# GpSimd takes over the small operations of a layer norm, and VectorE takes its row sums in halves

## What is computed

```python
xn = (x - mean(x)) / sqrt(var(x) + 1e-5)
Q, K, V = relu(xn @ Wq + bq), relu(xn @ Wk + bk), relu(xn @ Wv + bv)      # 16 heads of 16
mask = sign(abs(sum(xn, axis=-1)))                                        # of a row, as key and as query
attn = softmax(where(causal and mask of the key, Q K^T / 4, -2**32)) * mask of the query
a = attn @ V + xn ; a = gamma * layernorm(a) + beta
ffn = shared_expert(xn) + sum over the 2 best of 8 experts(xn), weighted
out = x + a + ffn
```

## Time and profile before

| | us |
|---|---|
| median of 3 runs (lowest, highest) | 2234.32 (2233.48, 2238.47) |
| the profiled execution | 2235.82 |
| its span, first to last instruction | 2234.1 |
| busy in it: TensorE, VectorE, ScalarE, GpSimd | 1916.0, 1399.5, 1080.4, 1123.0 |
| mean granted TensorE clock | 0.945 of full |
| first phase, pass -3 to the barrier | about 10 to 1150 |
| passes 0 to 12 | 161.5 to 981.5 |
| median and profiled execution apart | 1.5 |

### The profile page before, as it was taken

How to read it: one execution, slowest core, us unless ns; L and a number is a source line. 1 busy time by engine, 2 the same in 40 slices (tenths; PEclk the granted TensorE clock), 3 DMA queues, 4 the chain that set the end, 5 groups by cost and what they waited for, 6 DMA issues and landing times. The chain is left out here.

```text
span 2234.1 us, 37281 instructions
## 1 busy us (share of the span) xinstructions
PE 1916.0 (86%) x13238; PEld 1378.0 (62%) x13238; DVE 1399.5 (63%) x2934; ACT 1080.4 (48%) x2048; POOL 1123.0 (50%) x935
## 2 busy tenths in 40 slices
PE   0478988898898888889658999999999999799997
PEld 0245544554455544455327888888888888577776
DVE  6577788778877787877404656565555633355554
ACT  0115555555455555555335666666666654122221
POOL 5444433544455434542324767777776753544331
PEclk9769999999999999999878999999999999899999
DMA  1654565566666665666254666666566653444341
GB/s 36 120 98 80 105 115 115 128 127 125 120 134 130 127 122 127 123 119 125 80 178 162 203 207 206 208 195 207 188 209 200 212 179 99 137 142 135 115 128 57
DMA packets 235375, 314.01 MB, mean 141 GB/s; under 512 B 18970, under 2 KB 200356, under 8 KB 229028
## 3 DMA queue, kind: packets, MB, share of 16 engines
q1 hardware_dynamic: 222948, 278.63, 50.2%
q0 software_dynamic: 12288, 33.57, 5.0%
HBM read 211.43 MB, written 100.70 MB: 140 GB/s over the span
## 5 line engine op out<-in xcount | busy, mean ns | idle before, releaser
L495 ACT ACTIVATE pT<-st_ps 128x512 f32<-128x512 f32 (+1 forms) x704 | 383.6, 559 | 481.7 <-PE st_ps L995 396.6
L1638 PE MATMUL gu<-xc,w_up_h 128*128 128x512 f32 x1760 | 556.2, 397 | 41.1 <-DVE hf L1528 18.7
L719 DVE TENSOR_REDUCE mx<-s_ps 128x1 f32<-128x512 f32 (+3 forms) x704 | 436.1, 637 | 157.5 <-PE s_ps L974 125.8
L972 PE MATMUL s_ps<-k_aug,q_aug 97*128 97x512 bf16 (+3 forms) x1024 | 296.5, 322 | 138.4 <-DVE mx L719 128.4
L1638 PEld LDWEIGHTS gu<-xc,w_up_h 128*128 128x128 f32 x1760 | 324.9, 190 | 127.7 <-issue 34.3
L1638 PE MATMUL gu<-xc,w_up_l 128*128 128x512 f32 x880 | 345.9, 393 | 0.4 <-issue 0.3
L1360 POOL TENSOR_TENSOR w_up_l<-w_raw,w_up_h 128x512 fp32r<-128x512 f32 x160 | 204.1, 1298 | 209.2 <-ACT w_up_h L1442 209.2
L993 PE MATMUL st_ps<-q_aug,k_aug 99*128 99x512 bf16 (+3 forms) x1024 | 288.2, 314 | 21.9 <-ACT pT L495 11.4
L972 PEld LDWEIGHTS s_ps<-k_aug,q_aug 97*128 97x128 bf16 x1024 | 102.6, 101 | 323.2 <-DVE mx L719 237.3
L1528 DVE TENSOR_TENSOR hf<-sil,gu 128x512 f32<-128x512 f32 x220 | 150.9, 686 | 231.3 <-ACT sil L1447 230.6
L411 POOL DMA_INDIRECT expert_rows<-xrow,slot x128 | 125.2, 978 | 314.9 <-DMA q_aug<-neg_scr 248.1
(11 more groups left out here) (206 smaller groups left out, 3423.5 us busy)
## 6 DMA issues: line engine op xcount, KB each, us to landing
w_raw<-in_L_ffn_w_dram SPq DMA_DIRECT2D x117, 512.0 KB, 6.1
part_scr<-parts SPq DMA_DIRECT2D x64, 384.0 KB, 9.4
q_aug<-part_scr SPq DMA_DIRECT2D x192, 128.0 KB
k_aug<-part_scr SPq DMA_DIRECT2D x192, 128.0 KB
xr<-expert_rows SPq DMA_DIRECT2D x39, 512.0 KB
expert_results<-yo SPq DMA_DIRECT2D x39, 512.0 KB, 3.3
x_sb<-in_L_attn_x_dram SPq DMA_DIRECT2D x16, 512.0 KB
layernorm_rows<-xn SPq DMA_DIRECT2D x16, 512.0 KB
```

The costliest lines, as they stand in the source:

```text
L495: fn(pT[:, j % 2, h:h + heads, 0:w], unit_view(st_ps[u % 2], heads, w), ACT.Exp).then_inc(exp_done, 1)
L719: vec.tensor_reduce(mx[:, q, h:h + heads], unit_view(s_ps[u % 2], heads, keys), AX_X, ALU.max).then_inc(s_max, 2)
L972: mm(v[:, n], q_aug[par][0:ROWS_S, h0 + n, P * q:P * (q + 1)], k_aug[par][0:ROWS_S, h0 + n, 0:keys], start=True, stop=False)
L1638: last = mm(gu[m % 2][:, a], w_up[wpar][x][:, a, c, P * m:P * (m + 1)], xc[par][:, y, c], start=k == 0, stop=k == 3 * NC - 1)
```

## The change

It moves the 128x4 arithmetic of the norm and the folds from VectorE to GpSimd, in six pieces: `small_mean` (fold and mean), `small_variance` (fold, mean, epsilon and the power), `small_step`, `small_root`, `small_parts` and `small_mask`. VectorE keeps the wide operations, the reciprocals (which it alone does here) and the bit masks. Every passing of the work between the two is a semaphore of its own. VectorE's three row sums become six instructions of half the width, each in a unit of its own. The units move: sums of x after 1 and 2, centring 4 (was 3), squares 13 and 14 (was 14), reciprocals 18, 20 and 23 (the root was at 18 and 20), quotient 25 and 27 (was 24 and 26), masks 40, 41 and 43 (was 41 and 42). Two fused operations (multiply and add in one) become two each on GpSimd, since it takes a tensor operand for every constant (`norm_consts`). `xn_ready` is renamed `mk_ready`.

```diff
-        AT_NORM = (1, 2, 3, 14, 15, 18, 20, 24, 26, 41, 42)
+        AT_MEAN, AT_CENTRE, AT_VAR = (1, 2), 4, (13, 14)
+        AT_R0, AT_R1, AT_RD, AT_QUOT, AT_BITS = 18, 20, 23, 25, 27
+        AT_MASKS = (40, 41, 43)
...
+            small_begin, small_mark, small_op, small_end = chain(pool, chain_small, 28)
+
+            def fold4(a, b, final):
+                small_op(gp.tensor_tensor(tree2[:], a, b, ALU.add))
+                t2 = tree2[:].rearrange("p t (a b) -> p t a b", b=2)
+                small_op(gp.tensor_tensor(tree3[:], t2[:, :, :, 0], t2[:, :, :, 1], ALU.add))
+                return gp.tensor_tensor(final, tree3[:, :, 0], tree3[:, :, 1], ALU.add)
...
+            def small_mean(b):
+                small_begin(b)
+                await_(pool, mean_part, 2 * (b + 1))
+                small_op(fold16(s[SUM]))
+                await_(pool, a_ready, b)
+                gp.tensor_tensor(s[MEAN], s[SUM], inverse, ALU.mult).then_inc(mean_ready, 1)
+
+            def small_variance(b):
+                await_(pool, var_part, 2 * (b + 1))
+                small_op(fold4(lanes[:, :, 0:4], lanes[:, :, 4:8], s[SUM]))
+                small_op(gp.tensor_tensor(s[T1], s[SUM], inverse, ALU.mult))
+                small_op(gp.tensor_tensor(s[V1], s[T1], eps, ALU.add))
+                gp.tensor_tensor(s[S0], s[V1], half[:], ALU.pow).then_inc(s1_ready, 1)
+
+            def small_step(b):
+
+                await_(pool, r0_ready, b + 1)
+                small_op(gp.tensor_tensor(s[Q1], s[V1], s[R0], ALU.mult))
+                small_op(gp.tensor_tensor(s[T1], s[Q1], s[S0], ALU.add))
+                gp.tensor_tensor(s[D1], s[T1], half[:], ALU.mult).then_inc(d1_ready, 1)
+
+            def small_root(b):
+
+                await_(pool, r1_ready, b + 1)
+                small_mark(gp.tensor_tensor(s[SL], s[D1], s[SH], ALU.subtract))
...
+                gp.tensor_tensor(s[ROOT], s[T1], s[D1], ALU.add).then_inc(root_ready, 1)
+
+            def small_parts(b):
+                await_(pool, root_ready, b + 1)
+                await_(pool, rd_ready, b + 1)
+                small_mark(gp.tensor_tensor(s[DL], s[ROOT], s[DH], ALU.subtract))
+                small_op(gp.tensor_tensor(s[NRD], s[RD], minus, ALU.mult))
+
+            def small_mask(b):
+                await_(pool, mask_part, 2 * (b + 1))
+                await_(pool, mk_ready, b)
+                fold16(s[MASK_SUM]).then_inc(mask_sum, 1)
+                small_end()
```

`fold16` is two additions and then `fold4`, five operations; `small_root` has eleven. Their places in GpSimd's `body`:

```diff
+                if norm:
+                    small_mean(i + 3)
                 for b in mine if one is None else []:
                     scatter(b, range(NT))
...
                 if norm:
-                    await_(pool, v1_ready, i + 4)
-                    gp.tensor_tensor(sm[:, 2], sm[:, 1], half[:], ALU.pow).then_inc(s1_ready, 1)
+                    small_variance(i + 3)
                 if project:
                     second(i + 2, 2)
+                if norm:
+                    small_step(i + 3)
                 if project:
                     second(i + 2, 3)
                     third(i + 2, 2)
+                if norm:
+                    small_root(i + 3)
                 if one is not None:
                     scatter(one, [2])
                 if project:
                     third(i + 2, 3)
                 if norm:
+                    small_parts(i + 3)
                     quotient(i + 3)
                 if one is not None:
                     scatter(one, [3])
+                if norm:
+                    small_mask(i + 3)
```

On VectorE:

```diff
+            def row_sums(rows_, h):
+
+                t_ = slice(2 * h, 2 * h + 2)
+                return vec.tensor_reduce(lanes[:, t_], rows_[:, t_].rearrange("p t (k l) -> p t l k", l=16), AX_X,
+                                         ALU.add)
+
+            def ln_mean(b, h):
+                if h == 0:
+                    await_(dve, x_in, 16 * (b + 1))
+                    await_(dve, mask_sum, b)
+                row_sums(x_sb, h).then_inc(mean_part, 1)
...
             def ln_centre(b):
-                ln(vec.tensor_scalar(sm[:, MEAN], sm[:, SUM], 1.0 / C, None, ALU.mult))
+                await_(dve, mean_ready, b + 1)
+                await_(dve, normed, b)
...
+            def ln_r0(b):
                 await_(dve, s1_ready, b + 1)
...
+                vec.reciprocal(s[R0], s[S0]).then_inc(r0_ready, 1)
+
+            def ln_r1(b):
+                await_(dve, d1_ready, b + 1)
+                vec.reciprocal(s[R1], s[D1])
+                vec.tensor_scalar(s[SH].bitcast(U32), s[D1].bitcast(U32), HIGH_BITS, None, ALU.bitwise_and
+                                  ).then_inc(r1_ready, 1)
+
+            def ln_rd(b):
+                await_(dve, root_ready, b + 1)
+                vec.reciprocal(s[RD], s[ROOT])
+                vec.tensor_scalar(s[DH].bitcast(U32), s[ROOT].bitcast(U32), HIGH_BITS, None, ALU.bitwise_and
+                                  ).then_inc(rd_ready, 1)
...
+            def ln_masks(b, h):
+                if h == 0:
+                    await_(dve, normed, b + 1)
+                row_sums(xn, h).then_inc(mask_part, 1)
...
             def ln_masks_end(b):
-                fold(lanes[:], sm[:, SUM], ln)
-                ln(vec.tensor_scalar(msk[:], sm[:, SUM], 0.0, None, ALU.not_equal))
+                mask_begin(b)
+                await_(dve, mask_sum, b + 1)
+                mask(vec.tensor_scalar(msk[:], s[MASK_SUM], 0.0, None, ALU.not_equal))
                 await_(dve, mk_ps, b)
```

More of the change, by code:

```diff
@@ L106, in attention_phase @@
         cmask = sb("cmask", [P, 2, P], BF16)
-        half = sb("half", [P, NT])
+        half, norm_consts = sb("half", [P, NT]), sb("norm_consts", [P, 3, NT])
         zeros = sb("zeros", [P, NT, C])
@@ L383, in _ @@
             gp.memset(one[:], 1.0).then_inc(consts, 1)
-            await_(pool, consts, 4)
+            for k, value in enumerate((1.0 / C, LN1_EPS, -1.0)):
+                gp.memset(norm_consts[:, k], value).then_inc(consts, 1)
+            await_(pool, consts, 7)
             gp.affine_select(out=identf[:], in_=identf[:], compare_op=ALU.is_equal, fill=0.0, base=0,
@@ L424, in third @@
                 gp.tensor_tensor(parts[:, 2, u], r1[:, u], parts[:, 1, u], ALU.subtract).then_inc(b2_done, 1)
+            s = [sm[:, k] for k in range(20)]
+            inverse, eps, minus = (norm_consts[:, k] for k in range(3))
+            small_begin, small_mark, small_op, small_end = chain(pool, chain_small, 28)
[4 more added lines that the diff above has]
+                return gp.tensor_tensor(final, tree3[:, :, 0], tree3[:, :, 1], ALU.add)
@@ new lines, in fold16 @@
+            def fold16(final):
+                v = lanes[:].rearrange("p t (a b) -> p t a b", b=4)
+                t1 = tree1[:].rearrange("p t (a b) -> p t a b", b=4)
+                small_mark(gp.tensor_tensor(t1[:, :, 0], v[:, :, 0], v[:, :, 1], ALU.add))
+                small_op(gp.tensor_tensor(t1[:, :, 1], v[:, :, 2], v[:, :, 3], ALU.add))
+                return fold4(t1[:, :, 0], t1[:, :, 1], final)
+            def small_mean(b):
[4 more added lines that the diff above has]
+                gp.tensor_tensor(s[MEAN], s[SUM], inverse, ALU.mult).then_inc(mean_ready, 1)
@@ new lines, in small_root @@
+            def small_root(b):
+                await_(pool, r1_ready, b + 1)
+                small_mark(gp.tensor_tensor(s[SL], s[D1], s[SH], ALU.subtract))
+                small_op(gp.tensor_tensor(s[REM], s[SH], s[SH], ALU.mult))
+                small_op(gp.tensor_tensor(s[T2], s[V1], s[REM], ALU.subtract))
+                small_op(gp.tensor_tensor(s[REM], s[SH], s[SL], ALU.mult))
+                small_op(gp.tensor_tensor(s[T1], s[REM], s[REM], ALU.add))
+                small_op(gp.tensor_tensor(s[T3], s[T2], s[T1], ALU.subtract))
+                small_op(gp.tensor_tensor(s[T2], s[SL], s[SL], ALU.mult))
+                small_op(gp.tensor_tensor(s[REM], s[T3], s[T2], ALU.subtract))
+                small_op(gp.tensor_tensor(s[T3], s[REM], s[R1], ALU.mult))
+                small_op(gp.tensor_tensor(s[T1], s[T3], half[:], ALU.mult))
+                gp.tensor_tensor(s[ROOT], s[T1], s[D1], ALU.add).then_inc(root_ready, 1)
@@ L647, in _ @@
-            s = [sm[:, k] for k in range(20)]
-            def ln_root(b):
-                await_(dve, s1_ready, b + 1)
-                ln(vec.reciprocal(s[R0], s[S0]))
-                ln(vec.tensor_tensor(s[Q1], s[V1], s[R0], ALU.mult))
-                ln(vec.tensor_tensor(s[T1], s[Q1], s[S0], ALU.add))
-                ln(vec.tensor_scalar(s[D1], s[T1], 0.5, None, ALU.mult))
-                ln_mark(vec.reciprocal(s[R1], s[D1]))
-                ln(vec.tensor_scalar(s[SH].bitcast(U32), s[D1].bitcast(U32), HIGH_BITS, None, ALU.bitwise_and))
@@ L675, in ln_quotient @@
             def ln_quotient(b):
+                ln_begin(b)
+                await_(dve, rd_ready, b + 1)
                 for i in range(NT):
@@ L678, in ln_quotient @@
                 ln(last)
```

(21 more changed lines are left out.)

104 lines of the change are left out of this document (36 added, 68 removed).

## The result

The changed kernel takes 2230.08 us, the median of 14 runs (2225.76 to 2235.58), against 2236.7 us for 14 runs of the kernel before that were taken with them. The ratio is 0.9969 with a 95% interval of 0.9958 to 0.998: faster by 0.31%, some 7 us. The forecast was 1.2%, 27 us. The sign and the range held; three quarters of the gain did not come.

What follows compares the result with a forecast made beforehand. No single engine bounds a pass: VectorE its ends, TensorE most units, a GpSimd chain units 13 to 17. Ten passes 17.5 us, early passes 10, pass -1 1, start -4, clock 2: 27 us off, 2207 us, range 2188 to 2238.

Steps and rivals of the forecast that it cites:

- The price of a link: One small chained operation on GpSimd costs 0.28 us with its pause, ends 0.28 and 0.46; on VectorE about 0.20.
- rival (a): GpSimd's links are longer than four trace rows say; at 0.46 us each, about 2252 us in all; chance 0.16.
- The wait at the mean: Units 0 to 4: VectorE waits 0.55 us for `mean_ready`, 1.75 us after the second half, two maxima covering 1.2.
- The pass's ends: Units 40 to 43 gain 0.9 us a pass; units 0 to 4 between nothing and 0.57, taken as 0.35.
- The cast of unit 17: Units 13 to 17: `second(2)` 0.7 us late, VectorE's cast back from 1.37 to 0.43 us; net gain 0.2.
- Passes 0 to 2 and the start: Passes without scatters gain about 3.4 us each, 2.2 in units 18 to 22; the unhidden first norm costs about 4.
- Units 5 to 12 ... are TensorE's: In the typical pass TensorE bounds units 5 to 12, busy 10.20 of 11.13 us; no gain or loss entered.
- Units 23 to 26: Gain of 0.3 us a pass, as two small operations go on to unit 23.
- Units 18 to 22: Some 3.3 us of VectorE's small operations leave or move on; TensorE bounds the typical pass, so no gain here.
- (b): TensorE's low-clock stretches fill what is given back; only units 40 to 43 and early passes pay: 2226 us, chance 0.14.
- (c): VectorE's relief of 6.6 us ends the low-clock stretches, passes near 57.8 us: 2186 us in all, chance 0.12.
- (d): VectorE isn't relieved, waiting for GpSimd as long as it worked; half so at unit 4, counted inside (a).

Runs made afterwards that it cites:

- first two experiments: GpSimd's scatter 0 and its wait moved from the stream's head to just before the quotient: on the changed kernel 2205.84 us, on the kernel before 2241.35 us.
- second experiment: Kernel before, with GpSimd's scatter 0 and its wait moved to just before the quotient: 2241.35 us, ratio 0.9991.
- eighth experiment: Kernel before with negated maxima loaded first on SyncE, scatters 0 and 1 heading GpSimd's stream, scatter 2 behind `third(3)`: 2167.3 us, ratio 0.995.
- third experiment: Changed kernel with GpSimd's scatter 2 put behind `third(3)` instead of ahead of it: 2226.38 us, ratio 0.9913.
- first and fourth experiments: Changed kernel, with scatter 0 moved to just before the quotient: 2205.84 us; with SyncE's negated maxima ahead of its fourteen loads: 2205.36 us.
- seventh experiment: Changed kernel with negated maxima loaded first on SyncE, scatters 0 and 1 heading GpSimd's stream, scatter 2 behind `third(3)`: 2110.51 us, ratio 0.969.

## Why the prediction held, and where it failed

The mechanism of the gain was right, and its price too. What the forecast lacked was a wait that the gain itself would bring about, and a collision.

**The price of a link: right.** It was put at 0.28 us with its pause. After, by line over 100 to 982 us (busy, mean ns | idle before):

```profile
L439 POOL TENSOR_TENSOR tree<-tree 128x8 f32<-128x8 f32 x43 | 8.7, 202 | 3.4
L445 POOL TENSOR_TENSOR tree<-lanes 128x16 f32<-128x16 f32 x29 | 6.4, 219 | 86.1 <-DVE lanes L692 84.0 <-issue 2.1
```

202 ns and 0.08 before each; with 16 columns 219, and 0.27 on average for the dearest (L489). The first link of a chain costs no more than the others, so rival (a), for which the 0.38 of the earlier trace rows spoke, is out.

**The wait at the mean: right in size.** Forecast 0.55 us:

```profile
719.26 0.22 POOL L445 TENSOR_TENSOR tree<-lanes 128x16 f32<-128x16 f32 x1 [4.47 <-DVE lanes L692]
...
720.83 1.14 DVE L705 TENSOR_SCALAR ln_a<-x_sb,sm 128x256 f32<-128x256 f32 x4 [0.46 <-POOL sm L454]
```

The six links take 719.26 to 720.80, the wait is 0.46. What was not seen is that the halves create it: a second half in unit 2 is done one unit later than a whole sum in unit 1. With whole sums the wait is gone and the stage takes 5.95 us. The second instruction of a split sum costs 0.14 us (2.01 against 1.87), not "at most 0.1".

**The pass's ends: right in kind, too small in size.** Units 40 to 43 were put at -0.9 and gave -1.14; units 0 to 4 at -0.35 and gave -0.84, more than the 0.57 that was to be the most. The step from 0.57 to 0.35 was taken for the low clock of 0.77; after, the granted clock in these units is 1.00. Where the rest above 0.57 comes from I have not traced.

**The cast of unit 17: right.** It came down from 1.37 to 0.42 us:

```profile
746.52 0.42 DVE L769 CAST parts<-r 128x512 bf16<-128x512 f32 x1
```

The net of -0.2 for units 13 to 17 can't be read off the changed kernel: they start 3.6 us late, GpSimd's chain having had that time, and take 8.72 us at a clock of 0.81. The first two experiments show it, since scatter 0 is out of the way in both: 10.34 us with the change and 10.65 without it, -0.3.

**Passes 0 to 2 and the start: right.** 3.4 us each was said and 4.0 measured; the stretch of units 18 to 22 that was to lose 2.2 of its 8.74 us lost 3.1 (8.74 to 5.68). The start was to cost 4; the first unit of pass -1 came 4.8 later (102.1 to 106.9). Pass -1 gave back 3.6, where 1 was said.

**"Units 5 to 12 ... are TensorE's": the step that failed.** It was true of pass 8 of the kernel before, and was carried over as if it would stay true, with nothing put down for these units in the sum. I cut units 5 to 12 as one stretch, saw 10.20 of 11.13 us busy, and listed the waits of the engines that were late, not of those that were early. GpSimd's 194.4 us of waiting for `neg_loaded` (ten times, up to 23.5 us) was in the same view as the earlier trace rows:

```profile
POOL expert_rows L411 <- DMA q_aug<-neg_scr: 194.4, 10, 23.5
```

It looked like the idle time of an engine that isn't the bound. It is in fact the end of a chain of 17.5 us that starts at one point of the pass and is awaited at another, with a slack of 1.41 us at `second(1)` and none at `second(0)`. The forecast took 1.25 us out of the pass around these two points (0.9 and 0.35) and nearly 2 came (1.14 and 0.84), and it never asked what would wait when the work got there earlier.

The loss can be added up, from pass 8 before to pass 9 after, of which this is the stretch of units 10 to 12:

```profile
728.71:736.84 8.13, 4.50 (x42) 2.39 (x39) 2.87 (x5) 4.59 (x9) 4.53 (x5) 0.96 0.54 163
```

It is 3.8 us longer than the 4.33 of before. VectorE's cast of unit 11 starts 6.38 us after unit 10 (728.71 to 735.09) instead of 3.48 (679.43 to 682.91), so 2.9 later. Of these, 1.7 come from the start of the chain, which now falls 1.7 us and not 3.4 ahead of the pass; 0.8 from units 0 to 9, which take 13.3 us instead of 14.1; 0.4 from the chain itself. The last 0.9 is the cast, 1.36 us instead of the 0.43 of the earlier trace rows: `second(1)` no longer has to wait for `qf` and runs beside it. On GpSimd the slack absorbs its share: `second(1)` starts 1.4 us late (6.3 us after unit 10, at 735.0, instead of 4.9), so that a part of the 3.8 us is made up for in units 13 to 17, which hang on GpSimd. Removing the chain gave back 2.0 to 2.2 us a pass (63.26 to 61.23 and 61.11).

The kernel before had shown the chain at work. Its pass 13, the one without a norm, lost some 4 us to it. These are units 10 to 12 of that pass, in the kernel before and in the same kernel with scatter 0 moved (second experiment):

```profile
992.58:1001.07 8.49, 4.49 (x42) 2.39 (x39) 2.87 (x5) 4.59 (x9) 4.50 (x5) 0.94 0.28 95
```

```profile
995.05:999.37 4.32, 4.32 (x42) 2.40 (x39) 2.01 (x4) 3.05 (x6) 1.15 (x1) 1.00 0.32 107
```

So the pass that the prediction took as its cap, 57.8 us, had some 4 us of the very chain in it that then took the gain. With the order mended and no other change, pass 13 takes 52.2 us (eighth experiment), and full passes with the change get below the supposed cap (57.0 with whole sums).

**Units 23 to 26: wrong sign.** 0.3 us of gain was put there. The text saw that `third(3)` would come up to 3 us later and asked only who reads its tile. It did not ask what would run beside it. That costs 1.05 us in this pass, some 10 us in all; the third experiment gives it back.

**Units 18 to 22: too careful.** Put at nothing for the typical pass on account of the clock of 0.77; they gave 1.64, at 1.00. The caution was not groundless: with the chain out of the way the low clock is back there in half of the passes (first and fourth experiments).

**VectorE's busy time: down by 77 us, not by about 100.** Of the difference 15 us are the quotient's multiplies, which are held up beside `third(3)` (29.7 us after, 14.7 before).

**The rivals.** (b) named 2226 and 8 us of gain, and the whole time is close to it, but not for its reason: the granted clock over passes 3 to 12 rose from 0.94 to 0.96, the time was lost in units 10 to 12 and 23 to 26, and edits of order brought it back. That the number fits is luck. Its mechanism exists, though: where only the chain was removed, the lower clock took 1.5 us of units 18 to 22 back in half of the passes. (c), passes near 57.8 us, is what the change gives with all three edits of order (57.8 in the seventh experiment), and the low-clock stretches go with it, as (c) had it: the granted clock over passes 3 to 12 is 0.99. (d), VectorE waiting for GpSimd, came true in form, 44.1 us of waiting for `r`; but GpSimd was itself waiting for a DMA and not at work.

**What stays open.** Pass 13 took 57.9 us before, 59.9 after, 63.2 with scatter 2 moved and 53.3 with the negated maxima first. The 2 us between the first two are the chain again (units 10 to 12 take 8.49 before and 10.43 after), but in some runs units 27 to 39 of this pass take 17.1 to 17.5 us instead of 13.9, and pass 14 lost 1.9 (70.5 to 72.4); neither is traced. Scatter 1 was moved only together with the other two edits, so its own share of units 13 to 17 is not known.

## What to carry to other kernels

When an edit makes a loop shorter, look for the chains whose length it doesn't change, DMA chains above all: take each long wait of an engine off the bound, follow it to where it starts and to who is queued behind it, and write down the slack at its end. What an edit takes out between the two points beyond this slack is not gained there, however much work is taken away. A small transfer that somebody waits for goes ahead of the large ones on an in-order queue, and when an operation is delayed, ask what it will run beside as well as who reads it. And when a pass serves as the cap of a forecast, look at what bounds that pass first.

## What the runs showed of the hardware

A store of 16 KB took 1.4 us from issue to the issue of the load that waits for it when it went first, and 7.5 to 9.0 us behind fourteen loads on the same queue. Beside a GpSimd operation on 512 columns (1.16 us), some of VectorE's operations are held up, large or small: the cast goes from 0.42 to 1.37 us, four multiplies of 256 columns from 1.13 to 2.63, and an operation on four columns, which takes 0.14 us alone, to 0.56. Others are not: in the kernel before the row maxima over 512 columns, read from PSUM, take 0.68 us on average both beside these operations and away from them, and a reciprocal on four columns 0.16 beside them and 0.18 away. The operation on four columns:

```profile
749.03 0.56 DVE L722 TENSOR_SCALAR sm<-sm 128x4 uint32<-128x4 uint32 x1
...
754.38 0.14 DVE L728 TENSOR_SCALAR sm<-sm 128x4 uint32<-128x4 uint32 x1
```

GpSimd's chained additions on 4 to 16 columns cost nearly the same, 0.20 to 0.22 us and 0.08 between them; the dearest small operation of this phase took 0.27 on average.
